# Adding to stored rows by indirect sends, and moving two steps at the end of a hybrid attention and expert kernel

## The reference, cut to what matters

```python
t = _to_tokens(x)                              # x after the neighbourhood attention
t = t + _L1_attn_ref(_ln_t(t), ...)            # h = tanh(q_i + k_j + bh); e = h . Wa; softmax over j; sum a v
t = t + _L1_ffn_ref(_ln_t(t), ...)
...
# _L1_ffn_ref, T = 2048 tokens, C = 320 slots for each expert
idx = jnp.argmax(probs, axis=-1)
pos = (jnp.cumsum(one_hot, axis=0) * one_hot).sum(-1).astype(jnp.int32) - 1
kept = pos < C
buf = jnp.zeros((E, C, D)).at[idx, pos_safe].set(x, mode='drop')
hmid = jax.nn.relu(jnp.einsum('ecd,edf->ecf', buf, w1) + b1[:, None, :])
ybuf = jnp.einsum('ecf,efd->ecd', hmid, w2) + b2[:, None, :]
y_tok = ybuf[idx, pos_g] * (prb * kept)[:, None]
y = jnp.nan_to_num(y, nan=0.0, posinf=10000.0, neginf=-10000.0)
```

## Time and profile before

| | |
|---|---|
| median of 3 runs | 666.19 us (665.96 to 670.08) |
| profiled execution, its own time | 666.21 us |
| its span | 664.4 us |
| busy share of the span | PE 81%, DVE 73%, ACT 87%, POOL 73% |
| mean granted clock of PE | 0.964 |
| moved by DMA | 24.65 MB in 14236 packets |

### The profile page before, as it was taken

One profiled execution on the slowest core, in us unless ns is written; L12 is line 12 of the kernel. 1 busy time (PEld: TensorE's weight loads), 2 busy tenths in 40 slices (PEclk: granted clock), 3 DMA queues, 4 the chain that ended last, 5 costly groups with the idle time before them and its releaser, 6 DMA issues.

```text
span 664.4 us, 12448 instructions
## 1 busy us (share of the span) xinstructions
PE 536.7 (81%) x4545; PEld 266.3 (40%) x4545; DVE 486.2 (73%) x1372; ACT 578.8 (87%) x417; POOL 487.1 (73%) x585
## 2 busy tenths in 40 slices
PE   9999879998989889986967966676686667776993
PEld 6666533343444334443323312222231222336872
DVE  3767677879888877786678897877868787833455
ACT  3777599999999999999999999999999999960540
POOL 1004688988979768979989997979888797911474
PEclk9999998999999989999879999989989999997997
DMA  9700100100000000005300000000000000003300
GB/s 317 239 1 2 65 1 5 61 1 5 10 5 10 5 0 14 11 5 204 162 0 13 9 5 13 1 14 9 4 9 5 13 0 14 7 4 100 81 27 28
DMA packets 14236, 24.65 MB, mean 37 GB/s; under 512 B 1296, under 2 KB 11058, under 8 KB 13152
## 3 DMA queue, kind: packets, MB, share of 16 engines
q1 hardware_dynamic: 12768, 20.96, 9.2%
q0 software_dynamic: 1408, 2.91, 1.3%
HBM read 17.12 MB, written 7.37 MB: 37 GB/s over the span
## 4 chain that ended last, share of the span: by engine, by line
PE 32%; issue 22%; ACT 21%; DVE 18%; POOL 5%; DVEq 0%; POOLq 0%; ACTq 0%
ACT front L1268 18%; PE ps L967 7%; DVE front L1562 3%; PE ps L1148 3%; PE ps L758 3%; POOL front L628 3%; PE ps L806 2%; PE ps L1152 2%; PE ps L787 2%; PE ps L1004 2%; DVE back L1377 2%; DVE back L1404 1%; PE ps L797 1%; POOL x_one L605 1%; PE ps L873 1%
## 5 line engine op out<-in xcount | busy, mean ns | idle before, releaser
L628 POOL TENSOR_SCALAR front<-k,q 128x1024 f32<-128x1024 f32 (+1 forms) x424 | 388.1, 934 | 43.8 <-PE ps L967 36.3
L1268 ACT ACTIVATE front<-front 128x4096 f32<-128x4096 f32 (+1 forms) x125 | 418.7, 3398 | 1.4 <-POOL front L628 0.8
L967 PE MATMUL ps<-front,cst 128*32 128x512 f32 x2032 | 254.2, 621 | 72.6 <-ACT front L1268 65.6
L1562 DVE TENSOR_SCALAR front<-ps,q 128x512 f32<-128x512 f32 x218 | 188.3, 902 | 19.8 <-PE ps L967 16.5
L967 PEld LDWEIGHTS ps<-front,cst 128*32 128x32 f32 x2032 | 55.3, 112 | 188.2 <-issue 97.6
L1194 ACT ACTIVATE back<-back,mn 128x320 f32<-128x320 f32 (+1 forms) x128 | 62.7, 542 | 9.6 <-DVE mn L1377 9.6
L1377 DVE CUSTOM_DVE_ANT_0 back<-ps,back 128x320 f32<-128x320 f32 (+1 forms) x128 | 54.0, 469 | 10.3 <-PE ps L758 8.9
L1594 DVE COPY ptm<-ps 128x512 f32<-128x512 f32 x31 | 21.4, 692 | 37.6 <-PE ps L993 35.9
L1256 ACT ACTIVATE front<-k,q 128x1024 f32<-128x1024 f32 (+1 forms) x50 | 46.2, 956 | 2.1 <-DVE k L1673 2.1
L575 POOL TENSOR_TENSOR lnw<-lny,lnh 128x4 f32<-128x4 f32 (+1 forms) x9 | 1.8, 200 | 57.7 <-DVEq L1537 52.4
L758 PE MATMUL ps<-conv 32*128 32x320 f32 (+1 forms) x256 | 38.4, 472 | 1.6 <-DVE mn L1377 1.3
(11 more groups left out here) (164 smaller groups left out, 673.1 us busy)
## 6 DMA issues: line engine op xcount, KB each, us to landing
back<-in_w SPq DMA_DIRECT2D x2, 2048.0 KB, 11.0
xbuf<-rec SPq DMA_DIRECT2D x1, 2720.0 KB, 21.8
back<-in_top SPq DMA_DIRECT2D x2, 1024.0 KB, 5.8
back<-in_bottom SPq DMA_DIRECT2D x2, 1024.0 KB, 9.0
front<-xbuf SPq DMA_DIRECT2D x2, 720.0 KB, 6.7
back<-in_inner SPq DMA_DIRECT2D x1, 1280.0 KB, 9.9
back<-in_b SPq DMA_DIRECT2D x1, 1280.0 KB, 15.9
xT<-in_xT SPq DMA_DIRECT2D x4, 256.0 KB, 5.8
```

What stands on the lines that cost most here:

```text
L628: last = nc.gpsimd.tensor_scalar(ring[u % DEPTH][:, at + lo:at + hi], k4[:, img * L + k0 + lo:img * L + k0 + hi], q4[:, m:m + 1], 1.0, ALU ...
L967: last = nc.tensor.matmul(bank(to)[c * U:(c + 1) * U, :], c_("wa", U - QPG - QPG * row, 2 * U - QPG - QPG * row), ring[t % DEPTH][:, at:at ...
L1268: last = nc.scalar.activation(ring[t % DEPTH][:, 0:to], ring[t % DEPTH][:, 0:to], ACT.Tanh)
L1562: last = nc.vector.tensor_scalar(ring[u % DEPTH][:, at + lo:at + keys], ps[:, base + k0 + lo:base + k0 + keys], q4[:, m:m + 1], None, ALU.add)
```

## The change

Four things are changed. The indirect sends no longer write whole rows but add to the rows that stand in the output (`compute_op=ALU.add`); so DVE's addition of the residual rows goes, and the loads of the records shrink from 144 to 16 columns. They come in three parts (tiles 0 to 4, 5 to 9, 10 to 19) where there were two, and the weights, exponentials and token numbers are worked out in these three parts. The phases of block 14 move one more step ahead. And the first five slot tiles are turned by PE between block 15's logits and its counts, where they stood at the head of `place_slots`; the six filler products behind them go.

```diff
@@ phase_step
-    return PEND[p] + 1 + phase - (0 if p != NB - 2 else 1 if phase < 8 else 2)
+    return PEND[p] + 1 + phase - (0 if p != NB - 2 else 2 if phase < 8 else 3)
@@ sync
             fetch(xe, 5, 10, 0, C, ld_xe[1])
-            fetch(xr, 0, 10, C, REC, ld_xr[0])
+            fetch(xr, 0, 5, 2 * C, REC, ld_xr[0])
+            fetch(xr, 5, 10, 2 * C, REC, ld_xr[1])
             fetch(xe, 10, TILES, 0, C, ld_xe[2])
-            fetch(xr, 10, TILES, C, REC, ld_xr[1])
+            fetch(xr, 10, TILES, 2 * C, REC, ld_xr[2])
@@ gpsimd
             def weighted_bias(q):
-                pool.wait_ge(prb_ready, 1 + q // 2)
+                pool.wait_ge(prb_ready, min(q, 2) + 1)
@@
                 nc.gpsimd.indirect_dma_start(out_d, bass.IndirectOffsetOnAxis(ap=dest[:, k:k + 1], axis=0),
-                                             ye[:, k, :], None, bounds_check=NT - 1,
-                                             oob_is_err=False).then_inc(out_st, 16)
+                                             yf[:, k, :], None, bounds_check=NT - 1, oob_is_err=False,
+                                             compute_op=ALU.add).then_inc(out_st, 16)
@@
-                if k in (0, 10):
-                    pool.wait_ge(dest_ready, 1 + k // 10)
+                if k in (0, 5, 10):
+                    pool.wait_ge(dest_ready, 1 + k // 5)
@@ tensor
+            def turn_first_slots():
+
+                pe.wait_ge(ld_xe[0], 16)
+                for k in range(PLACED):
+                    nc.tensor.matmul(bank(4 + k // 3, k % 3 * P, (k % 3 + 1) * P), xe[:, k, :], c_("ident"),
+                                     start=(k % 3 == 0), stop=False)
@@
                 if p is not None:
                     logits(t, p)
+                if p == NB - 1:
+                    turn_first_slots()
@@
             def place_slots():
 
-                pe.wait_ge(ld_xe[0], 16)
-                for k in range(PLACED):
-                    nc.tensor.matmul(bank(4 + k // 3, k % 3 * P, (k % 3 + 1) * P), xe[:, k, :], c_("ident"),
-                                     start=(k % 3 == 0), stop=False)
-                keep_clock(6, 3)
                 pe.wait_ge(xn_ready, NB)
@@ scalar
             for e in range(NE):
                 if e + 1 < NE:
                     rectified(e + 1)
+                if e == 0:
+                    gate_exps(0)
                 if e % 2 == 0 and e + 2 < NE:
                     turned_slots(e // 2 + 1)
                 if e < 2:
-                    gate_exps(e)
+                    gate_exps(e + 1)
@@ vector
-                    link(nc.vector.scalar_tensor_tensor(fill[:, 0:n, :], y, 0.0, clip[:, 0:n, :], ALU.min, ALU.max))
-                    link(nc.vector.copy_predicated(fill[:, 0:n, :], good[:, 0:n, :], y))
-                    nc.vector.tensor_tensor(y, fill[:, 0:n, :], xr[:, group[0]:group[0] + n, 0:C],
-                                            ALU.add).then_inc(y_out, n)
+                    link(nc.vector.scalar_tensor_tensor(fill, y, 0.0, clip[:, 0:n, :], ALU.min, ALU.max))
+                    nc.vector.copy_predicated(fill, good[:, 0:n, :], y).then_inc(y_out, n)
@@
             weights(0)
             for e in range(NE):
                 slots_out(e)
-                if e == 0:
-                    weights(1)
+                if e < 2:
+                    weights(e + 1)
```

More of the change, by code:

```diff
@@ L46 @@
 TILES = NE * CAP // P
+PARTS = ((0, 5), (5, 10), (10, TILES))
 HALF = CAP - 2 * P
@@ L331, in program @@
         o += TILES * C
-        xr = front[:, o:o + TILES * (REC - C)].rearrange("p (n c) -> p n c", n=TILES)
-        o += TILES * (REC - C)
+        xr = front[:, o:o + TILES * (REC - 2 * C)].rearrange("p (n c) -> p n c", n=TILES)
+        o += TILES * (REC - 2 * C)
         xeT = front[:, o:o + NE * CAP]
@@ L339, in program @@
         o += TILES * C
-        clip, fill, good = (front[:, o + i * 3 * C:o + (i + 1) * 3 * C].rearrange("p (n c) -> p n c", n=3)
-                            for i in range(3))
+        yf = front[:, o:o + TILES * C].rearrange("p (n c) -> p n c", n=TILES)
+        o += TILES * C
+        clip, good = (front[:, o + i * 3 * C:o + (i + 1) * 3 * C].rearrange("p (n c) -> p n c", n=3)
+                      for i in range(2))
         good = good.bitcast(U32)
-        assert o + 9 * C <= DEPTH * QPG * L
+        assert o + 6 * C <= DEPTH * QPG * L
         back = sb("back", [P, NH * (KEYS[TOP] + KEYS[INNER]) + 5 * NG * PW])
@@ L443, in program @@
         centred, place_ready, ld_count = sem("centred"), sem("place_ready"), sem("ld_count")
-        ld_xe, ld_xr = [sem(f"ld_xe{i}") for i in range(3)], [sem(f"ld_xr{i}") for i in range(2)]
+        ld_xe, ld_xr = [sem(f"ld_xe{i}") for i in range(3)], [sem(f"ld_xr{i}") for i in range(3)]
         xeT_done, xeT_ready = sem("xeT_done"), sem("xeT_ready")
@@ L1324, in rectified, with gate_exps @@
                                          bias=c_("b1", e * FC + c, e * FC + c + 1)).then_inc(h_out, 1)
[L1326 to L1329, removed]
+            def gate_exps(i):
+                lo, hi = PARTS[i]
+                act.wait_ge(ld_xr[i], 16)
+                nc.scalar.activation(lge[:, lo:hi, :], xr[:, lo:hi, 0:NE], ACT.Exp).then_inc(ge_ready, 1)
             turned_slots(0)
@@ L1807, in _, with weights @@
                     dve.sem_inc(t_ready[3], 1)
[L1809 to L1813, removed]
+            def weights(i):
+                lo, hi = PARTS[i]
+                dve.wait_ge(ld_xr[i], 16)
+                nc.vector.tensor_copy(dest[:, lo:hi], xr[:, lo:hi, NE]).then_inc(dest_ready, 1)
+                dve.wait_ge(ge_ready, i + 1)
                 link(nc.vector.tensor_reduce(zg[:, lo:hi], lge[:, lo:hi, :], AX, ALU.add))
@@ L1829, in slots_out @@
                     n = len(group)
-                    y = ye[:, group[0]:group[0] + n, :]
+                    y, fill = (t[:, group[0]:group[0] + n, :] for t in (ye, yf))
                     dve.wait_ge(ye_ready, group[-1] + 1)
```

## The result

The changed kernel is slower. Median 670.95 us (15 runs, 667.53 to 675.65) beside 667.49 us for the kernel before (15 runs); ratio **1.0057**, 95% interval 1.0043 to 1.0071. The forecast was 662.9, its range 658.0 to 670.0; the result lies 1 us above that range. It is within the 1% called no change in the forecast, but the interval lies wholly on the slower side. The profiled execution took 671.76 us, with a span of 669.9.

A forecast was written before the change was run, and what follows sets the result against it. It took ACT's tanh as the bound up to 590 us, then a chain through PE's products to POOL's sends. From 666.2, -1.1 - 4.8 + 1.35 + 0.2 - 0.65 + 0.8 + 0.9 = -3.3 gave 662.9 us, range 658.0 to 670.0.

The forecast's parts named there:

- The sends: POOL's sends at the end: adding to memory rows makes each 0.1 us longer, within 0 to 0.98; loss 0.8.
- that formula: Price of d more per send on POOL: 8 d while 12 d stays under 2.2, and 20 d - 2.2 beyond.
- signs of being wrong: Sends over 1.6 apart, PE waiting for the tiles before the counts, or the clock staying down past 612.
- first rival: The sends on POOL become the bound: at 0.49 more per send the time is 669.7; chance 0.15.
- Block 14: After the last energies: counts and DVE block leave the chain, attention product at about 596.0, not 597.15; gain 1.1.
- ACT covers both, and I take 0: Block 14's norm on POOL and attention product on PE pass other work; ACT hides the delays, cost 0.
- First tiles: Turned in PE's gap before block 15's counts, load landing in 3.3; placing starts at 606.4; gain 4.8.
- They just hide: The ten turning passes before the counts take 1.25 at full clock, 602.55 to 603.8, without delaying the counts.
- The clock: PE's clock around placing and first expert products: a 3.4 us dip loses 1.7, less 0.35; loss 1.35, between -0.35 and +1.95.
- Loads: Tiles 5 to 9 land at 612.0, PE wants them at 612.2; ACT awaits short records; loss 0.2, 0 to 1.7.
- DVE's sum: Each group loses its addition on DVE; only the group of tiles 12 to 14 is on the path; gain 0.65.
- Landing: Behind the last send, memory rows must be read before the sum is written; 0.9 loss, from 0 to 1.8.

The follow-up runs named there:

- the kernel with filler: Both moves with plain sends, plus filler products in PE's two idle stretches, against the kernel before: 661.83 us, ratio 0.9931.
- turning alone: Only the turning of the first tiles in the gap, no filler behind it, on the kernel before: 664.33 us, ratio 0.9958.

## Why the prediction was wrong

**The step that failed** is "The sends": "I take 0.1, about the distance of those two rows, since nothing but the operation changes." Measured 0.57, of which 0.42 doesn't depend on the number of rows sent, by the line through 64 and 128. The two instructions that the 0.1 was taken from, plain send and scatter, differ in bytes. Bytes are not what the addition changes, so their distance said nothing about it. The true size lay inside the stated 0 to 0.98, and past the 0.31 from which I had said that the sends decide. The mechanism of that formula held: the sends became one row that sets the end, 20 x 0.57 - 2.2 = 9.2 in place of 0.8, which turns 662.9 into 671.3. That the profiled execution took 671.76 is partly luck. Its last unit on ACT began 1.6 later than in the profile that the sum was made against; with the tails alone it would be 666.2 + 3.9 = 670.1. And other errors cancel within the 671.3: the clock cost 1.6 more than the sum had, landing and loads 1.0 less, and the row from first to last send, 41.3, was by my reckoning of the forecast's steps some 1.5 shorter. Two of the signs of being wrong that the forecast names came true: sends over 1.6 apart (1.86), and the clock down past 612 (614.4). So the first rival was the right one, with 0.15 of chance and a price taken at 0.49. The reason I gave for 0.49, a third descriptor per row, is not borne out: rows carry a quarter of the price. The Trainium skill (DMA: Bandwidth & Descriptors, Rules for kernel authors) says that an accumulate reads its destination and writes it later. No row here shows that reading by itself; from the last send to the end of the span it can have added no more than about 0.1.

**Block 14.** The 1.1 is in the trace: from the end of PE's last energies to the attention product it is 3.5 (594.14 to 597.65, rows above), before 4.6 (592.53 to 597.15):

```profile
597.15 2.07 PE ps L1004 x16
```

"ACT covers both, and I take 0" held in 12 of 13 profiles and cost 1.9 in one. I had missed that PE's turning of the normed rows queues ahead of energies and would wait 2.25 for POOL, and that the clock falls behind that wait.

**First tiles.** The load landed in 3.07 (3.3 forecast). "They just hide" failed: at half clock ten passes took 2.31, and the counts came about 0.8 late. With the clock held they do hide: ten passes took 1.38, and the counts followed 0.16 behind them. Turning and filler at their old place were 4.8 as said.

**The clock.** I took a dip of 3.4 with 1.95 as the upper bound; it was some 10 us here. Against the kernel with filler, turning and counts lost 0.9, placing 1.0 and the first sixteen passes 1.4, in all 3.3, where the sum had 1.7. I had reasoned from the first gap's new work and the second gap's length, and left out that PE still idled 1.1 in the first gap before the load came. Whether that idle time is what brought the early fall is not shown: with turning alone PE idled 1.24 there, and the clock held until 608.

**Loads.** No wait of PE for tiles 5 to 9 shows: 0 instead of 0.2. **DVE's sum:** the addition's row is gone. The tails put the gain at 1.1 (75.3 less the 1.9 of late energies, against 74.5 with the addition) where the sum had 0.65; that pair also differs in the loads of the records, so the share of each isn't shown. **Landing:** 3.36 against 3.25: 0.1 instead of 0.9.

## What to carry to other kernels

An indirect DMA that adds cost only about 0.1 us more at the landing here, but 0.57 us more of POOL for each send. Price one adding send in a trace before letting twenty of them replace a vector addition of which only one group (0.56 us) was on the path. When a move puts work into an idle stretch, look at the granted clock behind it, and fill what is left of the idle time: by the tails the clock's fall cost 2.7 of the 5.9 us that the two moves were worth. And compare tails from a common event where the part ahead of the edit varies by more than the edit is worth.

## What the runs showed of the hardware

An adding indirect DMA of 128 rows takes POOL 1.55 us against 0.98, of 64 rows 1.41 against 0.92. With 128 rows the adding send takes the same 1.55 for rows of 256 and of 512 bytes. It makes one packet more for each row more, where the plain one's count was the same for 64 and for 128 rows. From the last send to the end of the span it took 3.36 us against 3.25.
